# Moving the layer-norm tail of two of four streams of the last tile onto VectorE

## What is computed

```
x = x + ln(attention(ln(x)))                 # 16 heads of 16 channels, causal, output projection
h = ln(x)
for blk in range(3):                         # two 256x256 linear layers with low-rank parts
    y = gelu(ln(linear_a(h)) * gamma + beta)
    h = linear_b(y) + h
x = x + ln(h)
```

## Time and profile before

| | |
|---|---|
| Runs | 1245.55, 1249.2, 1248.01 us |
| Profiled execution | 1250.09 us, of which the span from first to last instruction is 1248.3 us |
| TensorE (PE) busy | 1202.1 us, 96% of the span |
| ScalarE (ACT) busy | 1095.4 us, 88% |
| VectorE (DVE) busy | 770.1 us, 62% |
| GpSimd (POOL) busy | 435.0 us, 35% |
| Mean granted TensorE clock | 0.989 of full |

### The profile page before, as it was taken

One profiled execution on the slowest core, in us unless ns is written; L12 is line 12 of the kernel. 1 busy time (PEld: TensorE's weight loads), 2 busy tenths in 40 slices (PEclk: granted clock), 3 DMA queues, 4 the chain that ended last, 5 costly groups with the idle time before them and its releaser, 6 DMA issues.

```text
span 1248.3 us, 29297 instructions
## 1 busy us (share of the span) xinstructions
PE 1202.1 (96%) x10981; PEld 499.3 (40%) x10981; DVE 770.1 (62%) x1904; ACT 1095.4 (88%) x1251; POOL 435.0 (35%) x1373
## 2 busy tenths in 40 slices
PE   8999999999999999999999999999899999999967
PEld 6556434333333333333333333333333333333346
DVE  6775225566657667665674554675677666656466
ACT  4765999999999999999999999999899998999822
POOL 3221235442334444322462132245323145222144
PEclk9999999999999999999999999999899999999979
DMA  5985544554443544454544333456344354432100
GB/s 165 311 312 179 181 138 121 163 175 123 123 136 109 167 137 135 123 149 131 152 142 119 107 108 118 109 151 169 113 121 121 88 151 139 122 103 56 43 14 18
DMA packets 163246, 166.78 MB, mean 134 GB/s; under 512 B 91782, under 2 KB 125084, under 8 KB 163100
## 3 DMA queue, kind: packets, MB, share of 16 engines
q1 hardware_dynamic: 158812, 160.61, 43.8%
q10 hardware_dynamic: 4288, 4.26, 1.1%
HBM read 121.29 MB, written 39.32 MB: 129 GB/s over the span
## 4 chain that ended last, share of the span: by engine, by line
PE 51%; DVE 12%; POOL 7%; SPq 6%; DMA 5%; issue 4%; ACT 4%; DVEq 0%; POOLq 0%; ACTq 0%
PE O L1517 23%; PE S L1499 16%; PE F L209 10%; ACT probs L1442 4%; SPq L595 3%; DMA feed_mem<-turns 3%; DMA qkv_mem<-turns 2%; DVE stC L1611 1%; SPq L1357 1%; DVE feed_mem L1727 1%; DVE feed_mem L1728 1%; POOL tmpC L1390 1%; POOL tmpC L1391 1%; DVE feed_mem L1758 1%; SPq L1354 1%
## 5 line engine op out<-in xcount | busy, mean ns | idle before, releaser
L1442 ACT ACTIVATE probs<-S 128x1024 f32<-128x1024 f32 x1056 | 993.3, 1036 | 57.9 <-PE S L1499 52.7
L1517 PE MATMUL O<-probs,vg 128*32 128x512 f32 (+3 forms) x4608 | 537.7, 566 | 6.6 <-DVE o_turned L1675 3.1
L1499 PE MATMUL S<-q_op,k_op 64*128 64x512 f32 (+3 forms) x2304 | 377.6, 420 | 3.5 <-ACT probs L1442 2.4
L1499 PEld LDWEIGHTS S<-q_op,k_op 64*128 64x128 f32 x2304 | 178.8, 185 | 314.1 <-ACT probs L1442 250.3
L1517 PEld LDWEIGHTS O<-probs,vg 128*32 128x32 f32 x4608 | 112.7, 109 | 215.0 <-issue 192.0
L1420 POOL TENSOR_SCALAR_AFFINE_SELECT probs<-probs 128x512 f32<-128x512 f32 (+1 forms) x160 | 89.8, 572 | 164.0 <-ACT probs L1442 163.6
L1390 POOL TENSOR_SCALAR tmpC<-mvC 128x2 f32<-128x2 f32 x84 | 26.6, 316 | 301.2 <-DVE rstdC L1620 299.6
L209 PE MATMUL F<-wfT,feed_mem 128*32 128x256 f32 x960 | 62.4, 382 | 6.9 <-DVEq L1660 3.9
L1429 POOL TENSOR_TENSOR feed_mem<-feed_mem 128x512 f32<-128x512 f32 x30 | 32.2, 1073 | 104.9 <-DVE feed_mem L1716 104.8
L1758 DVE TENSOR_SCALAR feed_mem<-feed_mem,rstdC,nmrC 128x256 f32<-128x256 f32 x80 | 34.7, 475 | 55.1 <-POOL nmrC L1401 54.2
L1727 DVE SCALAR_TENSOR_TENSOR feed_mem<-feed_mem 128x512 f32<-128x512 f32 x90 | 63.2, 703 | 4.6 <-DVE feed_mem L1736 0.8
(11 more groups left out here) (212 smaller groups left out, 1257.9 us busy)
## 6 DMA issues: line engine op xcount, KB each, us to landing
k_op<-qk_rows SPq DMA_DIRECT2D x256, 256.0 KB, 3.7
qk_rows<-parts SPq DMA_DIRECT2D x32, 512.0 KB, 5.3
q_op<-qk_rows SPq DMA_DIRECT2D x128, 128.0 KB, 3.0
turns<-feed_mem SPq DMA_DIRECT2D x200, 64.0 KB, 1.9
feed_mem<-turns SPq DMA_DIRECT2D x50, 256.0 KB, 2.9
k_op<-qk_rows SPq DMA_DIRECT2D x48, 128.0 KB, 2.6
turns<-qkv_mem SPq DMA_DIRECT2D x80, 64.0 KB, 1.9
qkv_mem<-turns SPq DMA_DIRECT2D x20, 256.0 KB, 3.1
```

The costliest lines, as they stand in the source:

```text
L1442: nc.scalar.activation(probs[:, n % NP, :, :], S[:, n % NS, :, :], ACT.Exp, scale=SCALE).then_inc(exp_ok, 1)
L1499: last = nc.tensor.matmul(S[:, n % NS, a, at:at + TT - q0], k_op[mine, c % RING, pair, k0:k0 + P], q_op[mine, v % QS, pair, q0:TT], start= ...
L1517: last = nc.tensor.matmul(O[h * STRIP:(h + 1) * STRIP, q0:TT], vg[:, kb, col:col + STRIP], probs[:, n % NP, a, at:at + TT - q0], start=fir ...
```

## The change

The odd streams get what the even ones have: `rs` is the power alone; Newton step, normalisation and additions go to VectorE. The estimate of `rs` in `plan()` becomes 0.6 us for all four.

```diff
@@ runs_on
-    if t == NT - 1 and (name.startswith("copy") or k % 2 and name.startswith(("norm", "sc"))):
+    if t == NT - 1 and name.startswith("copy"):
         return "ACT"
-    if t == NT - 1 and (name.startswith("rs") or k % 2 and name in ("add_x", "result")):
+    if t == NT - 1 and name.startswith("rs"):
         return "POOL"
@@ plan
-                time = (SQUARE_POOL if ... (1.5 if k % 2 else 0.6) if name.startswith("rs") else 0.8) if eng == "POOL" else ...
+                time = (SQUARE_POOL if ... 0.6 if name.startswith("rs") else 0.8) if eng == "POOL" else ...
@@ GpSimd's root
-                    power = nc.gpsimd.tensor_tensor(r, r, minus_half[:, :], ALU.pow)
-                    if k % 2 == 0:
-                        return power
-                    link(s, power)
-                    link(s, nc.gpsimd.tensor_scalar(w, r, r, v, ALU.mult, ALU.mult))
-                    link(s, nc.gpsimd.tensor_scalar(r, w, 1.5, r, ALU.add, ALU.mult))
-                    return nc.gpsimd.tensor_scalar(nmr[:, b], mv[:, b, 0], -1.0, r, ALU.mult, ALU.mult)
+                    return nc.gpsimd.tensor_tensor(r, r, minus_half[:, :], ALU.pow)
@@ ScalarE's list
-                    elif name.startswith(("norm", "sc")):
-                        inputs_done(act, name, t, k)
-                        if name == "sc_att":
-                            stored_before(act, t, k)
-                        src = xC[:, t % 2, rows(t, k), :] if name == "norm_x" else normed(name, t, k)
-                        b = slots(t, k)
-                        last = nc.scalar.activation(own(y, t, k)[:, 0, :], src[:, 0, :], ACT.Identity, bias=nmr[:, b], scale=rstd[:, b])
-                        last.then_inc(act_ok[lane(t, k)], 1)
```

More of the change, by code:

```diff
@@ L1034, in plan @@
                 chain = (name, t, k)
-                time = (SQUARE_POOL if name.startswith("sq") else ROOT_POOL if t < NT - 1 else (1.5 if k % 2 else 0.6) if name.startswith("rs") else 0.8) if eng == "POOL" else 0.9 if t == NT - 1 and eng == "DVE" and name.startswith(("norm", "sc")) else short if t == NT - 1 else time
+                time = (SQUARE_POOL if name.startswith("sq") else ROOT_POOL if t < NT - 1 else 0.6 if name.startswith("rs") else 0.8) if eng == "POOL" else 0.9 if t == NT - 1 and eng == "DVE" and name.startswith(("norm", "sc")) else short if t == NT - 1 else time
                 item((name, t, k), eng, time, found, -1 if eng == "SP" else 1 if deps[0] in STEPS else 2)
```

## The result

The changed kernel took 1253.26 us (median of 11 runs, 1249.23 to 1254.43), the kernel before beside it 1248.57 us (11 runs). The ratio is 1.0033, 95% interval 1.002 to 1.0046: 4.1 us slower, 2.5 to 5.7 (the two medians lie 4.7 apart). The prediction had 1249.5 in a range that ended at 1252.5, and "within 0.3%" at 0.8. It was wrong in both.

A forecast was written before the change was run, and what follows sets the result against it. VectorE becomes the fullest engine in the last tile (52.0 us of work); the stages summed to its end at 1247.2 instead of 1245.8, 1.5 us slower, laid on the median 1248.01: 1249.5 us, range 1246.0 to 1252.5.

The forecast's parts named there:

- within 0.3%: Whole kernel: the time stays within 0.3% (3.7 us), what a measurement can tell from no change; chance 0.80.
- step 1: Last tile's att and x norms: TensorE resumes at 1202.9, 3.7 us later than now; `first0` 1 done at 1206.5.
- step 2: Block 0: clock back after 4.3 us, norm 4 ends at 1214.6, table load costs nothing, `first1` 1 done at 1218.2.
- step 3: A full block of the last tile: 11.4 us, against 10.57 now; `first2` 1 done at 1229.6.
- the lost pairing: Last tile's order: equal estimates end running streams 1 and 3 ahead, which hid one pair's norms beside the other's products.
- step 4: After norm 4 at 1237.4: four times ln_h, sc_h, result (2.24) and one exposed power, 9.6 us, to 1247.0.
- step 5: GpSimd's last power falls beside VectorE's additions: 0.2 us more (bounds 0 and 0.5), VectorE ends at 1247.2.
- A: Last tile: VectorE packs well and causes of idle and half clock go; gain stops at 3.1 us, 1244.9; chance 0.2.
- B: Blocks: TensorE's gaps make the clock fall, at most 1.6 us each; three falls give 1254.3; chance 0.15.
- C: Last tile: nothing moves, TensorE's order stays near the old, VectorE's additions hide in its slack; 1248.0; chance 0.1.
- D: Last tile: VectorE is nearly full (52.0 of 58.3 us), the change reverses advice to unload it; the forecast, chance 0.55.
- 2.2 us of waits that I missed: Whole kernel: such waits, or two or more clock falls, make it slower by over 0.3%; chance 0.17.

The follow-up runs named there:

- paired: The changed kernel with the old order, streams 1 and 3 again planned ahead of 0 and 2: tail 61.5 us, 1252.77 us, ratio 1.0029.
- end_order: The changed kernel with only VectorE's last twelve parts reordered, each ln_h ahead of the sc_h that waits for the stream before: tail 58.55 us.
- after_packed: The changed kernel, engines kept, with the last tile's lists of all engines written out from a search: tail 54.3 us, median 1246.45 us, ratio 0.9987.
- start_order: The changed kernel with only VectorE's first twenty parts reordered, depth first by stream: tail 62.8 us.
- adds_packed: The kernel before with only streams 1 and 3's add_x and result additions on VectorE, last-tile lists packed: tail 50.9 us, 1243.29 us, ratio 0.9957.
- part_att_x: The kernel before with the change made only for sc_att, norm_x and add_x of streams 1 and 3: tail 57.75 us.

## Why the prediction was wrong

- *Start (step 1): right.* TensorE resumed 1198.99 - 1185.37 = 13.6 us after the landing, as computed (1202.9 - 1189.3). `first0` 1 was done 17.3 us after it, 17.2 computed.
- *Block 0 (step 2): mostly right.* The clock came back 4.5 us after the restart (I took 4.3), norm 4 ended at 25.5 us (25.3), the table load was hidden. `first1` 1 was done at 29.5, 28.9 computed: seconds 3 and 4 ran as one piece behind turn 4, so the last stream's way was longer than 2.3 us.
- *Full block (step 3): 0.4 us too short.* 1226.72 - 1214.89 = 11.8 us, 11.4 computed, for the same reason. Norm 4 of block 2 ended at 49.2 us, 48.1 computed. Its direction was right, its stated reason (the lost pairing) was not: `paired` is no faster, and its stretch of products is longer.
- *The end (step 4): the step that failed.* I wrote "four times ln_h, sc_h, result and a power exposed, 9.6 us". It took 11.07 us (1234.56 to 1245.63). The power is exposed not once but four times, 0.67 and three times 0.44 us, since VectorE's list has each sc_h right behind the ln_h or the addition that can't cover the power. These waits are 2.0 us, where the step had one of 0.65. For the blocks the sum followed VectorE's list, for the end it only added up durations. `end_order` gives 1.7 us back by the order of this list alone.
- *The port (step 5).* The last power took 0.66 us against 0.55, so 0.11, where I had put 0.2; but three powers paid it. The Trainium skill ("SBUF — State Buffer", Who interferes with whom) calls the shared port pair an exclusive lock, held for the whole instruction. Here the power begun at 1238.02 ended 0.4 us after the addition beside it, less than its usual 0.55, so at least a part of it ran beside the addition.
- *The sum.* 0.2 + 0.4 (block 0), 0.5 (blocks 1 and 2) and 1.25 (the end) are the 2.3 us between my 57.9 and the measured 60.3. The sign was right, the size 1.5 in place of 3.8 to 4.1 us. With it the case for "within 0.3%" fell. That the time left the range as well is in part the reference: 3.8 us laid on the 1248.01 of my sum would be 1251.8, inside it, but the kernel before now stands at 1248.57, and the changed kernel 0.9 us above that and the tail's 3.8.
- *Rivals.* A (VectorE packs well) didn't come about by the plan's order, though `after_packed` shows that its mechanism is there. B didn't: gaps of 1.0 us on TensorE within a block left the clock at 1.00. In `paired` the clock did fall, after a gap of 2.0 us. C didn't. D, that moving work onto an almost saturated VectorE is the wrong way, is what held: in every pair with the same kind of list the old engines were faster, by 1.0 to 5.0 us. That range, however, is set by the lists.
- *The range.* I had given "2.2 us of waits that I missed" and two falls of the clock together a chance of 0.17. The missed 2.3 us are the first of the two; the range's end, 3.0 us above the forecast, was drawn from the falls of the clock and left no room for waits beside them.

## What to carry to other kernels

When work moves between engines under a planner, two things change: the load and all lists. Read the new list to its very end and write down what each instruction waits for, since a sum of durations assumes that latencies are covered. And before moving work, check the planner's estimates against the trace: here correct durations alone shortened the tail by as much as the whole change lengthened it, 3 to 4 us, and a packed order by more.

## What was not expected

- An earlier restart of TensorE made the kernel slower (`start_order`, 62.8 against 60.3 us): with gaps of some 2 us between its first products the granted clock stayed at 0.50 for about 15 us after the restart, against 4.5 us where it worked without a break. That the gaps are the cause isn't shown: in the other kernels the same time lies between 2.8 and 8.1 us, and the 8.1 of `adds_packed` had one gap of 0.65 us in it.
- How long TensorE is idle doesn't decide alone whether the clock falls. In the kernel before it fell after 1.7 us and in `paired` after 2.0, but in `part_att_x` it stayed at 1.00 over 2.1 us and after them:

```profile
1206.10:1208.20 2.10, 0.00 (x0) 0.00 (x1) 1.93 (x11) 0.60 (x2) 1.79 (x6) 1.00 0.00 0
1208.20:1209.60 1.40, 1.39 (x8) 0.90 (x8) 0.82 (x4) 1.39 (x2) 1.19 (x3) 1.00 0.00 0
1210.60:1214.00 3.40, 3.40 (x20) 3.02 (x20) 1.71 (x9) 1.40 (x4) 0.55 (x1) 1.00 0.00 0
```

- A table load on ScalarE does not wait for the input of the activation behind it: it ran at 1203.91, the activation at 1207.68. An activation that stands ahead of it in the queue does delay it, as in the kernel before.
- What stays open: why the run times differ by 4.1 us and the tails by 3.8 (the interval holds both), and how near the packed lists of the old engines are to the best ones. For those of the change VectorE's floor answers it.
